# A recurrent kernel on one core: ScalarE's gate results go to two PSUM banks, and the update gate and y share one bank each

## The reference, cut to what matters

```
Xz, Xr, Xh = X @ Wxz.T + bxz, X @ Wxr.T + bxr, X @ Wxh.T + bxh        # all steps
def step(H, (xz, xr, xh)):
    Z = sigmoid(xz + H @ Whz.T + bhz)
    R = sigmoid(xr + H @ Whr.T + bhr)
    H_tilda = tanh(xh + (R * H) @ Whh.T + bhh)
    H_new = Z * H + (1 - Z) * H_tilda
    Y = H_new @ Whq.T + bhq
    return H_new, Y
out = x + Ys                                                           # [32, 256, 256], fp32
```

## Time and profile before

| | us |
|---|---|
| median of 3 runs | 524.92 |
| lowest, highest | 524.47, 526.99 |
| the profiled execution, its own time | 523.88 |
| its span, first to last instruction | 522.0 |
| TensorE matmuls busy | 510.2 (98%) |
| TensorE weight loads busy | 492.3 (94%) |
| ScalarE busy | 329.2 (63%) |
| VectorE busy | 317.6 (61%) |

### The profile page before, as it was taken

One profiled execution on the slowest core, in us unless ns is written; L12 is line 12 of the kernel. 1 busy time (PEld: TensorE's weight loads), 2 busy tenths in 40 slices (PEclk: granted clock), 3 DMA queues, 4 the chain that ended last, 5 costly groups with the idle time before them and its releaser, 6 DMA issues.

```text
span 522.0 us, 96066 instructions
## 1 busy us (share of the span) xinstructions
PE 510.2 (98%) x44184; PEld 492.3 (94%) x44184; DVE 317.6 (61%) x1929; ACT 329.2 (63%) x1800; POOL 0.2 (0%) x4
## 2 busy tenths in 40 slices
PE   8499999999999999999999999999999999999997
PEld 7499999999999999999999999999999999999997
DVE  1266666666666666666666666666666666666665
ACT  2266666666666666666666666666666666666665
POOL 0000000000000000000000000000000000000000
PEclk9999999999999999999999999999999999999999
DMA  5111121111111111111221111111111111111111
GB/s 176 29 51 45 50 55 46 50 55 45 51 55 45 51 54 45 52 54 45 53 53 45 55 51 45 54 51 45 55 50 45 55 51 45 55 50 45 55 50 51
DMA packets 57735, 27.63 MB, mean 53 GB/s; under 512 B 6784, under 2 KB 56832, under 8 KB 57728
## 3 DMA queue, kind: packets, MB, share of 16 engines
q1 hardware_dynamic: 56880, 26.70, 18.4%
q10 hardware_dynamic: 848, 0.83, 0.5%
HBM read 18.98 MB, written 8.52 MB: 53 GB/s over the span
## 4 chain that ended last, share of the span: by engine, by line
PE 96%; issue 2%; DMA 1%; SPq 0%; DVE 0%; ACT 0%; ACTq 0%; DVEq 0%
PE r_ps L244 34%; PE c_ps L244 28%; PE z_ps L244 23%; PE y_ps L244 11%; DMA whq_sb<-in_whq_dram 1%; SPq L114 0%; SPq L115 0%; SPq L116 0%; SPq L112 0%; DVE u_sb L230 0%; DVE o_sb L212 0%; DVE h_sb L235 0%; ACT c_sb L189 0%; DVE rh_sb L225 0%; ACT r_sb L179 0%
## 5 line engine op out<-in xcount | busy, mean ns | idle before, releaser
L244 PE MATMUL c_ps<-xt_sb,wx_sb 128*32 128x64 f32 (+1 forms) x4104 | 172.8, 225 | 1.5 <-issue 1.5
L244 PE MATMUL z_ps<-xt_sb,wx_sb 128*32 128x64 f32 (+1 forms) x4104 | 163.3, 220 | 0.0
L179 ACT ACTIVATE r_sb<-r_ps 128x32 f32<-128x32 f32 x512 | 91.3, 198 | 106.1 <-PE r_ps L244 98.7
L225 DVE TENSOR_TENSOR rh_sb<-r_sb,h_sb 128x32 f32<-128x32 f32 x512 | 89.8, 192 | 85.3 <-ACT r_sb L179 81.1
L244 PE MATMUL z_ps<-h_sb,whz_sb 128*32 128x32 f32 x8192 | 123.9, 198 | 2.2 <-issue 2.2
L244 PE MATMUL c_ps<-rh_sb,whh_sb 128*32 128x32 f32 x8192 | 122.6, 198 | 2.2 <-issue 1.9
L244 PE MATMUL y_ps<-whq_sb,h_sb 128*32 128x128 f32 x2064 | 113.5, 279 | 0.3 <-DVE h_sb L235 0.3
L244 PEld LDWEIGHTS z_ps<-h_sb,whz_sb 128*32 128x32 f32 x8192 | 108.7, 110 | 2.4 <-issue 2.4
L244 PE MATMUL r_ps<-xt_sb,wx_sb 128*32 128x64 f32 (+1 forms) x4104 | 108.2, 219 | 0.0
L230 DVE SCALAR_TENSOR_TENSOR u_sb<-z_sb,c_sb 128x32 f32<-128x32 f32 x512 | 75.2, 188 | 53.5 <-ACT c_sb L189 53.5
L244 PEld LDWEIGHTS z_ps<-xt_sb,wx_sb 128*32 128x32 f32 (+1 forms) x4104 | 101.1, 110 | 0.0
(11 more groups left out here) (27 smaller groups left out, 359.3 us busy)
## 6 DMA issues: line engine op xcount, KB each, us to landing
xt_sb<-in_xt_dram SPq DMA_DIRECT2D x130, 64.0 KB, 1.8
xres_sb<-in_xr_dram SPq DMA_DIRECT2D x130, 64.0 KB, 1.8
out_dram<-o_sb SPq DMA_DIRECT2D x130, 64.0 KB, 1.6
wx_sb<-in_wx_dram SPq DMA_DIRECT2D x3, 256.0 KB, 3.4
whr_sb<-in_whr_dram ACTq DMA_DIRECT2D x1, 256.0 KB, 5.0
whz_sb<-in_whz_dram ACTq DMA_DIRECT2D x1, 256.0 KB, 5.1
whh_sb<-in_whh_dram ACTq DMA_DIRECT2D x1, 256.0 KB, 5.6
whq_sb<-in_whq_dram SPq DMA_DIRECT2D x1, 256.0 KB, 6.4
```

The lines of the kernel that those rows point to most:

```text
L179: nc.scalar.activation(r_sb[:, o], r_ps[:, o, here], ACT.Sigmoid).then_inc(s_r[o], 1)
L225: nc.vector.tensor_tensor(rh_sb[:, k], r_sb[:, k], old[:, k], ALU.mult).then_inc(s_rh[k], 1)
L244: return nc.tensor.matmul(ps, weights, moving, start=start, stop=False, skip_group_check=True, **kw)
```

## The change

What it does:

- A new pair of PSUM banks, `act_ps`, takes the results of ScalarE: sigmoid of r goes to columns 0 to 31 of bank o, tanh of c to columns 32 to 63 of the same bank. `r_sb` and `c_sb` are gone, and VectorE reads r and c from PSUM. The rest of bank 0 is used once, for the last y (`y_end`).
- To make room, z of both parities lies in one bank, and y in one bank. Two engines may not be in one bank at a time, so there are new waits: TensorE waits for the sigmoid of z (`s_z`) before the x pieces of z; ScalarE waits for the last x piece of z (`s_xz_ps`, new) before it seeds z; TensorE waits for the seed of z at s = 0 already before the four z parts, and no longer before the x piece of z.
- The order of x pieces and y follows the step: at s = 0, three x pieces of c, two of z, three of r and no y; at s = 1, one of c, two of z, one of r and two y pieces. Both z pieces come behind the c parts. Over the two steps of a chunk there are as many pieces as before.
- The residual comes at the head of a step s = 0, and the seed of y moves from s = 1 to s = 0.

```diff
-        r_sb = sb("r_sb", [P, K, B])
-        c_sb = sb("c_sb", [P, K, B])
...
-        z_ps = [banks(f"z_ps{p}", 1) for p in range(2)]
-        y_ps = [banks(f"y_ps{p}", 1) for p in range(2)]
+        z_ps = banks("z_ps", 1)
+        y_ps = banks("y_ps", 1)
+        act_ps = banks("act_ps", K)
+        y_end = act_ps[:, 0, CS * B:CS * B + P]
...
-                    sp.wait_ge(s_res, c * CS + 2 * CS)
+                    sp.wait_ge(s_res, c * CS + CS)
...
                     for o in range(K):
                         act.wait_ge(s_r_ps[o], t + 1)
-                        nc.scalar.activation(r_sb[:, o], r_ps[:, o, here], ACT.Sigmoid).then_inc(s_r[o], 1)
+                        nc.scalar.activation(act_ps[:, o, 0:B], r_ps[:, o, here], ACT.Sigmoid).then_inc(s_r[o], 1)
...
-                    if s == CS - 1:
+                    if s == 0:
                         act.wait_ge(s_res, t + CS)
-                        seed_y(p).then_inc(s_seed_y, CS)
+                        nc.scalar.copy(y_ps[:, 0, 0:P], bq_sb[:]).then_inc(s_seed_y, CS)
                     for o in range(K):
                         act.wait_ge(s_c_ps[o], t + 1)
-                        nc.scalar.activation(c_sb[:, o], c_ps[:, o, here], ACT.Tanh).then_inc(s_c[o], 1)
+                        nc.scalar.activation(act_ps[:, o, B:2 * B], c_ps[:, o, here], ACT.Tanh).then_inc(s_c[o], 1)
...
                         seed(c_ps[:, :, W * p:W * p + W], N).then_inc(s_seed_c, CS)
+
+                        act.wait_ge(s_xz_ps, t + 1)
                         seed(z_view(p), Z).then_inc(s_seed_z, CS)
...
+                    if s == 0:
+                        residual(y_ps[:, 0, 0:P], p, i * 2 + p - PAD, i * (2 * DMA) + DMA)
+
                     for k in range(K):
                         dve.wait_ge(s_r[k], t + 1)
...
-                        nc.vector.tensor_tensor(rh_sb[:, k], r_sb[:, k], old[:, k], ALU.mult).then_inc(s_rh[k], 1)
+                        nc.vector.tensor_tensor(rh_sb[:, k], act_ps[:, k, 0:B], old[:, k], ALU.mult).then_inc(s_rh[k], 1)
...
-                    if s == 0:
-                        residual(p, i * 2 + p - PAD, i * (2 * DMA) + DMA)
...
-                    x_piece(q, N, pieces[0])
+                    x_piece(q, N, 3 * s)
                     if u > 0:
                         pe.wait_ge(s_h[1], t + 1)
+                    if s == 0:
+                        pe.wait_ge(s_seed_z, t + 1)
...
-                    x_piece(q, N, pieces[1])
-                    if s == 0:
-                        pe.wait_ge(s_seed_z, t + 1)
-                    x_piece(q, Z, pieces[0])
+                    if s == 0:
+                        x_piece(q, N, 1)
+                        x_piece(q, N, 2)
+                    else:
+                        pe.wait_ge(s_seed_y, t + 1)
+                        y_piece(y_ps[:, 0, 0:P], q, 0)
...
-                    x_piece(q, Z, pieces[1])
+
+                    pe.wait_ge(s_z, t + 1)
+                    for piece in pieces:
+                        xz_mm = x_piece(q, Z, piece)
                     if s == 0:
                         pe.wait_ge(s_seed_r, t + 1)
-                    for piece in pieces:
-                        x_mm = x_piece(q, R, piece)
-                    if s == CS - 1:
-                        x_mm.then_inc(s_xt_used, 1)
+                        for piece in range(2):
+                            x_piece(q, R, piece)
+                    else:
+                        xz_mm.then_inc(s_xz_ps, CS)
+                        x_piece(q, R, 3).then_inc(s_xt_used, 1)
                     pe.wait_ge(s_zh, t + 1)
                     for k, o in AHEAD[(u + 1) % SLOTS]:
                         r_part((u + 1) % SLOTS, k, o, zh_sb[:, k])
                     if s == 0:
-                        pe.wait_ge(s_seed_y, t + 1)
-                    y_mm = y_piece(q, s)
-                    if s == CS - 1:
-                        y_mm.then_inc(s_y_ps, 1)
+                        x_piece(q, R, 2)
+                    else:
+                        y_piece(y_ps[:, 0, 0:P], q, 1).then_inc(s_y_ps, 1)
```

48 lines of the change are left out of this document (24 added, 24 removed).

## The result

The change makes the kernel slower: 535.71 us (533.96 to 536.73, 4 runs) beside 525.42 (524.47 to 526.99, 4 runs) for the kernel before, a ratio of 1.0189 with an interval of 1.0169 to 1.0210. The forecast was 525.3 us, and the result lies above its range, which ended at 532.0. The profiled run took 533.96 us with a span of 532.0, 10.0 more than the 522.0 of the kernel before, its clock was granted at 0.997.

A forecast was written before the change was run, and what follows sets the result against it. TensorE's stream was taken to bound u = 1, 2, 3 except the c parts; these and all u = 0, ScalarE and VectorE. +2.3 - 1.9 = +0.4 us on the profiled 523.88, put on the median: 525.3 us, range 518.2 to 532.

The forecast's parts named there:

- The new wait for z: TensorE's z pieces held by the sigmoid of z: 0.012 us a step, +2.3 us over three steps of 64 turns.
- the second pass makes up a part: Inside a z piece: staggered tiles recover some of the hold, a reason for taking 0.012 us.
- The order of pieces at 0: TensorE's x and y pieces: same work in a new order, taken as 0, ends -0.02 and +0.02 us per chunk.
- The residual at 0: Ahead of R * H at s = 0: fits, cost 0; at u = 0 could lose up to 0.05 us, 3.2 us.
- The seed of z at 0: Before the z parts at s = 0: done in time with 0.01 us to spare, so cost 0.
- r and c through PSUM: ScalarE's write 0.03 us shorter per hand-over, bounded by 0.008 and 0.037; VectorE's PSUM read costs 0.
- the 536 us: Time if VectorE's PSUM source cost the skill's 65 ns: net 0.035 us in 256 + 64 hand-overs, 11 us.
- That the gain ends in the wait for z: At u = 1, 2, 3 c parts start up to 0.03 us earlier, but z pieces still wait for s_z: gain 0.
- The turn of the loop: At u = 0 both hand-overs count, limited by TensorE's loop turn: -0.03 us each, -1.9 us in 64.
- the second (VectorE pays for PSUM): Slower: reading r and c costs VectorE more than the write saves; +6.4 us, 531.3, upper end +12.8; chance 0.18.
- The first, no hold by z: Faster: s_z does not bind, so 0.025 us comes through in u = 1, 2, 3; -6.7 us, 518.2; chance 0.31.
- The third, that only the wait for z is left: PSUM write saves nothing visible; 0.012 us in 256 steps, +3.1 us, 528.0; chance 0.11.

The follow-up runs named there:

- before_wait_z: The kernel before plus one wait of TensorE for the sigmoid of z ahead of the z piece behind the c parts; 532.39 us, ratio 1.0143.
- order_only: The changed kernel's order, residual and seed of y, but r and c in SBUF, z in two banks, no wait for z; 527.89 us.
- z_k_outer: The changed kernel with the z parts looped k outside, so the waits for seed and h[1] sit on different matmuls; 533.23 us.
- sbuf_rc: The changed kernel with r and c written to SBUF tiles again, all else as changed; 533.69 us, ratio 1.0172 to the kernel before.
- r_first_sbuf: The changed kernel with r's x pieces ahead of z's behind the c parts, and r and c in SBUF; 528.69 us, ratio 1.0075.
- r_first: The changed kernel with r's x pieces ahead of z's behind the c parts, so other work precedes the wait for z; 524.76 us, ratio 0.9993.

## Why the prediction was wrong

The forecast was +0.4 us and the change cost +10. In ns over the kernel before, the causes beside each other (the wait for z from before_wait_z; the order from order_only, with u = 0 taken as u = 2; the second wait from z_k_outer against the changed kernel):

| | u=0 to 1 | 1 to 2 | 2 to 3 | 3 to 0 | turn |
|---|---|---|---|---|---|
| wait for z | +33 | +34 | +32 | +1 | +100 |
| order of pieces | +14 | +2 | +14 | +2 | +32 |
| second wait at the z parts | +2 | +1 | +18 | 0 | +21 |
| sum | +49 | +37 | +64 | +3 | +153 |
| the whole change | +52 | +34 | +64 | +2 | +152 |
| the residual, without the wait for z | +19 | 0 | 0 | 0 | +19 |

The columns add up within 3 ns without the residual. With the wait for z its 19 ns don't show: in sbuf_rc the first half of R * H starts 274 ns behind the sigmoid of R at u = 0 and in the changed kernel 235 ns, and both steps last 1979. Without the held wait the account closes too: 7817 before, 51 for order and residual and 10 for the second wait are the 7878 of r_first_sbuf.

- **The new wait for z, the step that failed most.** Mechanism, place and start of the loads were right: 0.05 to 0.06 behind the sigmoid's end. The size was 12 ns in the sum and is 33: 11 at the first matmul, as taken, and 22 in the piece. I had written that "the second pass makes up a part"; it adds to the wait. 3 x 64 x 0.033 = 6.3 us instead of 2.3.
- **The order of pieces at 0.** It costs 32 ns a turn, 2.0 us. The prediction's own count had it: at s = 0 five x pieces for three and a y piece are 0.60 for 0.58, and 0.02 a chunk is what its end allowed; measured are 16 ns a chunk. It took 0.
- **The residual at 0.** At u = 0 R * H does wait for it, since VectorE turns its own loop first; I had seen that and given this and the like a chance of 4%. Alone it costs 19 ns, 1.2 us, inside the end of 0.05; in the changed kernel nothing that shows.
- **The seed of z at 0.** It was in time, as the text said. But it makes a second wait at one matmul, and that costs 18 ns in the steps u = 2, 1.2 us, with no semaphore late (the seed ends 162 ns ahead of the loads). I had asked only whether the wait would be over.
- **r and c through PSUM.** 16 ns a hand-over instead of 30, inside my ends of 8 and 37, and VectorE pays 0, as its row of y had it; nor does R * H start later, by the medians it comes 32 ns behind the end of ScalarE's record in both kernels. The rule in the Trainium skill, "VectorE: DVE Perf Modes", its section on the TRN2 errata, by which the PSUM source would cost more, does not hold for this instruction: the earlier trace rows has 192 ns and the changed kernel 190. That the 536 us which the prediction worked out from it lie beside the measured 535.7 is chance, since sbuf_rc, which reads r and c from SBUF, has the same steps. The one in "ScalarE: Activation LUTs", Step-by-step: what each stage is for, agrees with the trace, by 198 to 182. That the gain ends in the wait for z was right (sbuf_rc: 1 ns).
- **The turn of the loop.** -30 ns forecast, +2 measured. The chain is shorter there as computed, but the u parts' loads stand behind the branch, and those come 25 ns later in the step than before, where I had allowed 0.01 for the wait for z. The wait alone moves them by 26 (before_wait_z), but so does the order alone (order_only), so why the branch is late stays open. Without the held wait the turn is 26 ns shorter (r_first), near the forecast.

Of the rivals, the second (VectorE pays for PSUM) had the right sign for a wrong reason: R * H starts 0.21 behind the sigmoid where it was 0.23, not later. The first, no hold by z, fell: the hold is there in every step. What it said of the gain behind it is true without the hold, in size 16 to 18 ns for 25. The third, that only the wait for z is left, was nearest in mechanism, but took 12 ns a step too.

Left open, beside the branch and the way of the residual's 19 ns: the step from u = 1 to 2 takes 25 ns more than its neighbours before (1952) and in before_wait_z (1986), the two kernels with the old order of pieces, and at most 13 ns more than a neighbour in those with the new one. And how the 14 ns at u = 2 divide over the passages from one kind of piece to the next was argued from medians, no run takes it apart.

## What to carry to other kernels

A wait put into the middle of a matmul stream can cost more than the time by which its semaphore is late (here 33 ns for 11): allow for the piece behind the wait that runs slower, and put a piece of independent work in front of it. When an engine shows 98% busy, a chain can still hold its instructions; take the time from one step's start to the next, and test the chain by making one hand-over shorter. Before work is moved to the head of a step, look at the one step in which its engine turns its loop.
